# Exponents between thirds of the counts, mixes by pairs of heads: a new order of TensorE's and ScalarE's queues in a top-64 attention kernel

## The reference, cut to what matters

```python
x = x + tanh(g_xattn[0]) * xattn(layernorm(x), ctx)       # x, ctx: (32, 256, 256)
x = x + tanh(g_ffn[0]) * ffn(layernorm(x))

# xattn: 16 heads of dimension 16; per batch entry and head 256 queries by 256 keys
Q = (q @ Wq.T + bq).reshape(b, 16, 256, 16)               # K and V likewise
scores = einsum('bhqd,bhkd->bhqk', Q, K) / sqrt(16)
topk_scores, topk_idx = top_k(scores, 64)
probs = softmax(topk_scores)
out = einsum('bhqk,bhqkd->bhqd', probs, V[topk_idx]).reshape(b, 256, 256) @ Wo.T + bo

# ffn: one quantised 256 x 256 product
x_q = (x / s_in).astype(float8_e4m3fn);  k_q = (kernel / s_k).astype(float8_e4m3fn)
y = (x_q @ k_q) * (s_in * s_k) + bias
```

## Time and profile before

| what | value |
|---|---|
| median of 3 runs | 3370.18 us (3369.51 to 3372.18) |
| the profiled execution's own time | 3371.54 us |
| its span in the profile | 3369.0 us |
| DVE busy | 2658.7 us, 79% of the span |
| ACT busy | 2533.1 us, 75% |
| PE busy (matmul) | 1825.7 us, 54% |
| POOL busy | 982.2 us, 29% |
| chain that ended last | DVE 38%, ACT 25%, issue 16%, PE 15% |
| largest group of ACT | the counts L949, x3072: 1514.0 us |
| first and last start of L1288, x64 | 120.8 and 3266.6 us |

### The profile page before, as it was taken

How to read it: one execution, slowest core, us unless ns; L and a number is a source line. 1 busy time by engine, 2 the same in 40 slices (tenths; PEclk the granted TensorE clock), 3 DMA queues, 4 the chain that set the end, 5 groups by cost and what they waited for, 6 DMA issues and landing times.

```text
span 3369.0 us, 53804 instructions
## 1 busy us (share of the span) xinstructions
PE 1825.7 (54%) x9104; PEld 969.0 (29%) x9104; DVE 2658.7 (79%) x10774; ACT 2533.1 (75%) x8774; POOL 982.2 (29%) x1204
## 2 busy tenths in 40 slices
PE   3354566566545565634566466556556455364654
PEld 2122233233323333322333233333223232132222
DVE  2678888778888778887878888887888788888774
ACT  1777888787877788766877778887688688687882
POOL 6122332233323223322223232322233133232112
PEclk8566777666777767666766777777677677677677
DMA  4313333223332222331323332232333123331111
GB/s 71 48 28 48 58 53 52 42 47 61 53 60 45 53 50 49 59 51 29 56 48 61 51 53 51 50 54 48 51 61 57 29 52 57 51 56 33 33 24 45
DMA packets 451908, 166.58 MB, mean 49 GB/s; under 512 B 245616, under 2 KB 451440, under 8 KB 451520
## 3 DMA queue, kind: packets, MB, share of 16 engines
q1 hardware_dynamic: 451136, 162.38, 27.4%
q0 software_dynamic: 384, 0.33, 0.1%
HBM read 102.57 MB, written 59.24 MB: 48 GB/s over the span
## 4 chain that ended last, share of the span: by engine, by line
DVE 38%; ACT 25%; issue 16%; PE 15%; DVEq 2%; ACTq 1%; DMA 0%; POOL 0%; SPq 0%; POOLq 0%; another core or an unknown queue 0%
ACT act_junk L949 18%; PE ps_o L786 5%; DVE masked L1291 4%; DVE score_sb L1153 4%; DVE following L1302 3%; PE ps_a L714 3%; DVE masked L1467 3%; DVE masked L1296 3%; ACT unfit L984 2%; ACT pT_sb L993 2%; DVE masked L1371 2%; DVE x_res L1471 2%; DVE max L1369 2%; PE ps_e L767 2%; PE ps_a L716 2%
## 5 line engine op out<-in xcount | busy, mean ns | idle before, releaser
L949 ACT ACTIVATE act_junk<-score_sb,X 128x256 int8<-128x256 f32 x3072 | 1514.0, 504 | 136.3 <-DVE X L1247 69.2
L767 PE MATMUL ps_e<-qs,ks 99*128 99x256 bf16 x1024 | 353.7, 354 | 1351.3 <-ACT pT_sb L993 1349.5
L786 PE MATMUL ps_o<-pT_sb,v_aug 128*32 128x256 f32 x2048 | 768.9, 516 | 0.5 <-ACT pT_sb L993 0.5
L984 ACT ACTIVATE unfit<-score_sb,thr 128x256 bf16<-128x256 f32 x1024 | 464.4, 507 | 245.4 <-DVEq L1418 244.7
L1153 DVE TENSOR_SCALAR_CACHE_REDUCE score_sb<-ps_s 128x256 f32<-128x256 f32 x1024 | 409.8, 415 | 259.1 <-PE ps_s L753 258.7
L949 ACT ACTIVATION_READ_ACCUMULATOR act_junk<-score_sb,X 128x1 f32 x3072 | 606.5, 197 | 0.0
L767 PEld LDWEIGHTS ps_e<-qs,ks 99*128 99x128 bf16 x1024 | 123.5, 121 | 1444.9 <-ACT unfit L984 1346.3
L771 PE MATMUL ps_e<-dropb,unfit 128*128 128x128 bf16 x2048 | 362.2, 276 | 0.0
L993 ACT ACTIVATE pT_sb<-ps_e 128x512 f32<-128x512 f32 x512 | 303.9, 594 | 46.0 <-PE ps_o L786 46.0
L1291 DVE TENSOR_SCALAR_CACHE_REDUCE masked<-score_sb,X 128x256 f32<-128x256 f32 x768 | 318.9, 470 | 13.4 <-DVE x_res L1471 8.4
L786 PEld LDWEIGHTS ps_o<-pT_sb,v_aug 128*32 128x32 f32 x2048 | 233.1, 137 | 269.5 <-issue 199.5
(11 more groups left out here) (181 smaller groups left out, 3830.0 us busy)
## 6 DMA issues: line engine op xcount, KB each, us to landing
rows<-q_scr SPq DMA_DIRECT2D x192, 128.0 KB, 5.1
rows<-k_scr SPq DMA_DIRECT2D x192, 128.0 KB, 4.9
o_scr<-o_sb SPq DMA_DIRECT2D x128, 128.0 KB, 2.7
q_scr<-split SPq DMA_DIRECT2D x32, 384.0 KB, 2.7
k_scr<-split SPq DMA_DIRECT2D x32, 384.0 KB, 2.7
x_in<-in_x SPq DMA_DIRECT2D x32, 256.0 KB, 3.5
ctx_sb<-in_ctx SPq DMA_DIRECT2D x32, 256.0 KB, 3.6
v_scr<-proj SPq DMA_DIRECT2D x32, 256.0 KB, 5.9
```

The source lines that it names most:

```text
L767: nc.tensor.matmul(ps_e[:, n % 2, kc * TOK:(kc + 1) * TOK], ks[u][:, h, 8 * kc:8 * kc + 8, :].rearrange("d j t -> d (j t)"), qs[u][:, h, : ...
L786: ins = nc.tensor.matmul(ps_o[32 * c:32 * c + 32, half * TOK:(half + 1) * TOK], v_aug[p][:, 2 * h + kc, :], pT_sb[:, n % 2, kc * TOK:(kc + ...
L949: ins = nc.scalar.activation(act_junk[:, t, :], score_sb[:, slot, t, :], ACT.Sign, scale=-1.0, bias=X[slot % 2][:, 0, t:t + 1], accum_out= ...
L984: ins = nc.scalar.activation(unfit[:, n % MASKS, jh, :], score_sb[:, slot, t, :], ACT.Relu, scale=-1.0, bias=thr[:, slot, t:t + 1])
```

## The change

The order of three queues changes, with what it needs of buffers and semaphores:

- **ScalarE.** The 16 counts of a round are cut in thirds of 5, 5 and 6 (`THIRDS`). Ahead of each third stands one exponential, now three heads behind the masks (MIX_LAG = 3); in round 2 the third place is that of `evacuate_gauss`. The masks of a round stand together behind its counts, the evacuation of mixed heads ahead of the final counts. Each count now has a wait of its own, for the count four before it (`act_junk` has 4 places and no longer 16), and raises the semaphore itself.
- **TensorE.** A round is now: exponents, scores of its first and second head, exponents, [in round 0 the sum of unsure rows], scores of its third head, exponents, the larger product of the round, and last the mixing, for two heads at a time and with their matmuls interleaved. Scores are no longer one head ahead.
- **VectorE.** The third head's two copies stand ahead of the last step of `final_tiles`, and so ahead of the update. Nothing stands inside the update's chain any more but the final steps of round 2.
- `pT_sb` has four places and no longer two.

The core of the diff:

```diff
-MASK_LAG, MIX_LAG = 2, 4
+MIX_LAG = 3
+QUAD = 4
+PAIR = 2
+JUNK = 4
+THIRDS = ((0, 1, 2, 3, 4), (5, 6, 7, 8, 9), (10, 11, 12, 13, 14, 15))
...
+                pe.wait_ge(s_PT, H + PAIR)
+                pe.wait_ge(s_O, at(4 * b + 2 * g + half))
                 for kc in range(2):
-                    ins = nc.tensor.matmul(ps_o[32 * c:32 * c + 32, half * TOK:(half + 1) * TOK],
-                                           v_aug[p][:, 2 * h + kc, :], pT_sb[:, n % 2, kc * TOK:(kc + 1) * TOK],
-                                           start=(kc == 0), stop=(kc == 1), tile_position=(0, 32 * c))
-                ins.then_inc(s_PV, 1)
+                    for k in range(PAIR):
+                        n = PAIR * pair + k
+                        c = n % QUAD
+                        ins = nc.tensor.matmul(ps_o[32 * c:32 * c + 32, half * TOK:(half + 1) * TOK],
...
+                ins.then_inc(s_PV, PAIR)
...
+                    for r in range(GUIDES):
+                        taken(HEADS[r][0])
+                        next_scores(HEADS[r][0])
+                        next_scores(HEADS[r][1])
+                        taken(HEADS[r][1])
...
+                        if r == 0 and mixes:
+                            sum_unsure(2 * mb + mg, b - 2, b - 2 if g else b - 3)
+                        if r < 2:
+                            next_scores(HEADS[r][2])
+                            taken(HEADS[r][2])
...
-            def guide_counts(i, slot, r):
+            def guide_counts(i, slot, r, tiles):
+
+                for t in tiles:
+                    if t == 0:
+                        act.wait_ge(s_thr, GUIDES * i + r + 1)
+                        act.wait_ge(s_fc, at(4 * (i - 1) + 2 * r))
+                    act.wait_ge(s_cnt, at(GT * (GUIDES * i + r) + t - JUNK + 1))
...
                     for r in range(GUIDES):
+                        for k in range(3):
+                            if k < len(HEADS[r]):
+                                taken(HEADS[r][k])
+                            elif has(1):
+                                evacuate_gauss(2 * (b + 1) + g)
+                            if guided:
+                                guide_counts(2 * b + g + 1, (2 * p + g + 1) % RING, r, THIRDS[k])
                         if has(1) and (g, r) == (0, 0):
                             evacuate_moments(b + 1)
...
-                        next(finals)
                         copy(HEADS[r][1], 0)
                         copy(HEADS[r][1], 1)
+                        next(finals)
+                        if not last:
+                            copy(HEADS[r][2], 0)
+                            copy(HEADS[r][2], 1)
                         next(finals, None)
...
                         next(steps, None)
-                        for jh in range(2):
-                            next(ending, None)
-                            next(steps, None)
-                        for jh in range(2):
-                            next(ending, None)
-                            if not last:
-                                copy(HEADS[r][2], jh)
-                            next(steps, None)
                         for _ in ending:
                             next(steps, None)
```

More of the change, by code:

```diff
@@ L842, in _ @@
             key_moments(1)
-            scores(1, 1, 0, 0)
-            def mix_stage(b, p, u, g, n, before):
-                h = earlier(b, p, u, g, n, MASK_LAG, before)
-                if h:
-                    exponents(*h)
-                h = earlier(b, p, u, g, n, MIX_LAG, before)
-                if h:
-                    mix(*h)
             def batch(b, p, u, has):
@@ new lines, in lagged, with taken, next_scores @@
+                    def lagged(n):
+                        return earlier(mb, mp, mu, mg, n, MIX_LAG, has(-1)) if mixes else None
+                    def taken(n):
+                        if lagged(n):
+                            exponents(*lagged(n))
+                    def next_scores(n):
+                        if has(1):
+                            scores(b + 1, (u + 1) % OPS, g, n)
+                    for r in range(GUIDES):
[3 more added lines that the diff above has]
+                        taken(HEADS[r][1])
+                        if has(1) and r == 2:
@@ L888, in _ @@
+                        if has(-3) and (g, r) == (0, 2):
+                            ffn_matmul(b - 3)
             schedule(pe, batch)
@@ L1021, in _ @@
                     evacuate_values(0)
-            def mixing(b, p, u, g, n, before):
-                if n % 4 == 0 and before:
-                    done = earlier(b, p, u, g, n, GH, before)
-                    evacuate_mixed(done[0], done[3], n // 4)
-                h = earlier(b, p, u, g, n, MIX_LAG, before)
-                if h:
-                    exps(2 * h[0] + h[3], h[4])
             def batch(b, p, u, has):
@@ L1204, in start_thresholds @@
                 carry(dve)
[L1205 removed]
+                dve.wait_ge(s_fc, at(4 * (i - 1)))
                 carry(dve)
```

167 lines of the change are left out of this document (82 added, 85 removed).

## The result

The changed kernel takes 3224.1 us (median of 4 runs, 3222.2 to 3225.3) against 3369.9 of the kernel before (4 runs): ratio 0.9566, 95% interval 0.9549 to 0.9582, so 4.3% less. The prediction was 3276, range 3180 to 3375, faster with 72%. Direction, places and most sizes were right; the gain was put at 95 us and came as 146, half as much again. The profiled execution took 3223.6 us, span 3221.7, with a mean granted clock of 0.635 (before 0.703).

A forecast was written before the change was run, and what follows sets the result against it. A circle of waits between DVE, TensorE and ScalarE was to be cut; g = 1 was DVE's. Minus 2.2 us a batch, minus 68 over thirty, and minus 26 for settled rows gave 3276 us, range 3180 to 3375.

The forecast's parts named there:

- The waits for scores go: DVE's waits for scores inside the update: all 258.7 us go if nothing replaces them.
- The gate: Rounds 0 and 1: ScalarE's last six counts wait behind the third exponential, ending 8.85 and 8.55 us after round start.
- The chain of g = 0: Successive times through rounds 0 to 2 of half g = 0, with a 4.2 us moments wait; length 48.0 us.
- the two new waits: Half g = 1: DVE waits 0.9 us at the update in each of rounds 0 and 1.
- The collision term: Half g = 1: DVE's collisions with GpSimd partly leave update and finish, minus 2.3 us, bounds 0 and 5 kept.
- the prediction's own sign of being wrong: Among the signs listed as wrong: collisions in another place than update and finish.
- The prediction's variant in which all 5 us would stay: Half g = 1: later query copy meets round 1's merges and narrow tiles; 2.3 us a batch more, some 3346 us.
- What a batch was before: Length of a batch in the kernel before: mean of 96.3 and 93.3, taken as 94.8 us.
- Settled halves: 13 halves settle rows, about half with g = 0, where settling covers the new 4.2 us wait: minus 26 us.
- Rival 3: TensorE late: pairs don't overlap and the clock stays at 1.2 GHz; 2.7 us a batch more, 3357 us; 10%.
- Per-count waits: ScalarE's wait at each count: hidden, bounds 0 and 0.2 us; a rival with overlap undone, about 3570 us, 11%.
- the smaller form of 0.07 us a count: Smaller form of the slower-counts rival: 0.07 us a count for the register step, 3360 us; 8%.

The follow-up runs named there:

- e1: Changed kernel with TensorE's third-head exponents ahead of the third head's scores in rounds 0 and 1: 3056.2 us, 0.9065 of the kernel before.
- e3: Changed kernel with the edits of e1 and e2 together: 3054.0 us, 0.9061 of the kernel before.
- e2: Changed kernel with ScalarE evacuating the key moments at the start of a batch's first round: 3131.9 us, 0.9295 of the kernel before.
- e10: Kernel before the change with GpSimd's copy of queries or keys issued as four quarter copies: 3357.2 us, 0.9972 of the kernel before.
- e7: e3 with GpSimd's copy of queries or keys issued as four quarter copies: 3022.6 us, 0.8972 of the kernel before.
- e6: Changed kernel with each count waiting for the count just before it, not four back: 3396.6 us, 1.0084 of the kernel before.

## Why the prediction was right, step by step

The range was 195 us wide and would have held several mechanisms. What speaks for the predicted mechanism is the chain of times inside a half and e1 to e3, and not the sum, which missed a third of the gain.

- **The waits for scores go:** 258.7 to 7.8 us. Right.
- **The gate,** counts done 8.85 us after the start: measured 8.8; moments at 9.15, measured 9.14 with a wait of 4.09 where 4.2 was said. e1 and e2 show that it is this gate.
- **The chain of g = 0:** update 13.6 (13.55), round 1 at 19.5 (19.4), update 28.2 (28.0), update of round 2 at 42.4 (42.45), from there to the end 5.3 (5.5), length 47.7 here and 47.97 in the mean (48.0). In round 1 the wait for counts was 0.08 us, not 0.9: the narrow tiles met GpSimd there (L1334 x2 took 1.89 us, 0.87 without), which used up the wait. At the start values the wait was 3.45, not 2.6, with the same end.
- **g = 1:** the two new waits, said 0.9 each, are 1.10 and 1.03 in this half, 2.1 together in the mean; with them DVE's idle time grew by 2.2 us, where 2.1 was said. **The collision term was mis-sized:** I kept minus 2.3 between 0 and minus 5; DVE's busy time fell by 3.6 us a half (41.59 to 38.01). Together that is minus 1.4 (45.21 to 43.85) instead of minus 0.1. And the term isn't DVE's alone: e10 shows that such a relief is worth 0.4 us a half if TensorE stays late.
- **Where the collisions went:** GpSimd's copy of the queries starts 6.5 us later in the half, as said (about 6). By duration, finish takes 4.0 us less and the update's later steps 2.5 less; the narrow tiles, the merges, the update's first step and the first instruction of the half take 2.5 more. So the prediction's own sign of being wrong, collisions in another place than update and finish, did show, while the rest of the chain held. The prediction's variant in which all 5 us would stay (3346) did not come: a DVE operation with two tensors in SBUF does stand where it meets the copy (e7), but beside the copy DVE now mostly copies scores, looks for maxima or waits, and only its first update step stands:

```profile
1301.40 3.79 POOL L588 COPY qs<-rows 96x4096 bf16<-96x4096 bf16 x1
```

```profile
1301.66 0.41 DVE L1178 TENSOR_SCALAR_CACHE_REDUCE score_sb<-ps_s 128x256 f32<-128x256 f32 x1
...
1302.35 0.74 DVE L1341 MAX8 following<-masked 128x8 f32<-128x256 f32 x2
1304.12 1.10 DVE L1254 TENSOR_TENSOR X<-aim,count 128x16 f32<-128x16 f32 x1 [1.03 <-ACT act_junk L970]
```

- **What a batch was before:** I took 94.8 from two neighbouring batches; the mean over 22 and 23 halves is 95.4. With the last points this makes the gain 3.6 us a batch instead of 2.2: over the 45 steady halves 80 us instead of 49, 31 of the 53 us missed.
- **Settled halves:** the cover is right (e2: no change in them), and so is the size: the ten in the steady part brought 29 us, where the 26 for thirteen and the mean's gain make 31. All of it came in g = 0.
- **Start and end:** I gave them no more than the mean's gain, some 11 us with their settled halves; they brought 38, 27 more. The first entries lack DVE's extras; that they gained more because the circle alone bound them is argued, and no run tested it.
- **A slip in the sum:** 30 times 2.2 is 66, not 68; it changes nothing.
- **TensorE:** I put 2.2 us a pair at 1.2 GHz, 4.4 for the two, and held that just enough. A pair takes 1.92 there and two pairs side by side 1.95. The 1.31 us of the earlier trace rows were two heads that started one after the other; issued together, a pair takes 1.06 at 2.4 GHz (at 1268.3 us of the changed kernel, granted clock 1.00). Rival 3 had no ground.
- **Per-count waits:** free, as said, and the smaller form of 0.07 us a count does not show either (0.49 apart before and after). The price of an unmet wait is 0.145 us (e6), above the 0.08 from which I said that the change turns slower. With the gain that was really there it turns at 0.12: 0.145 cost 172 us, the gain was 146.

## What to carry to other kernels

Between engines with queues in order, ask of each wait what else stands behind it: here a swap of two lines, exponents ahead of scores that wait, was worth more (168 us) than the whole change before it (146). A cover works both ways: a stall that costs next to nothing beside a late neighbour is worth its full time once the neighbour is on time, so price both together. Take the length of a stage from all its repetitions, not from two.

## What the runs showed of the hardware

- A DVE operation with two tensors in SBUF that starts inside a copy of GpSimd of 96x4096 bf16 (3.8 us) stands until the copy ends, even a tiny one: in the changed kernel the first step of the update, 128x16, took 1.10 us beside it instead of 0.17. DVE's copies of scores out of PSUM (0.41) and its maxima (0.74 for two) kept their times beside the same copy. Four quarters take 4.37 us in all, and nothing at this place stood longer than 1.57 us beside them.
- Mixing matmuls for different quarters of TensorE's columns (128x32 weights, float32, granted clock 0.50 of full speed there, so 1.2 GHz) overlap almost wholly: four heads 1.95 us, two heads 1.92, one head 1.92, and for four heads in either of the two orders tried. The page "TensorEngine Tiling (Array Packing)" of the Trainium skill, section "Tiling Modes", says that tiles can load and multiply in parallel; the trace agrees, by these rows.
- ScalarE's counts with their sums start 0.49 us apart while each waits for one four back, and 0.635 apart when each waits for the one just before.
